# Routing that takes up a group's places after the next but one is finalised, and expert rows gathered four slots ahead

## What is computed

```python
x = x + gnn(layernorm(x), edges) + mix(layernorm(x))
y = layernorm(x)
logits = y @ gate_w + gate_b                      # [6250, 16]
topk_vals, topk_idx = top_k(logits, 2)
topk_w = softmax(topk_vals)
h = relu(y @ w1[e] + b1[e])                       # w1[e]: 256 x 512
expert_out = h @ w2[e] + b2[e]                    # w2[e]: 512 x 256
moe = sum(topk_w * expert_out of the two chosen)
x = x + layernorm(y + moe) * gamma + beta
```

## Time and profile before

| | |
|---|---|
| median of three executions | 2920.93 us |
| the profiled execution: its time, its span | 2916.77 us, 2915.0 us |
| TensorE matmul busy | 1810.2 us, 62% of the span |
| TensorE weight load busy | 1281.5 us, 44% |
| VectorE busy | 1755.7 us, 60% |
| ScalarE busy | 1404.4 us, 48% |
| GpSimd busy | 1329.1 us, 46% |

### The profile page before, as it was taken

One profiled execution on the slowest core, in us unless ns is written; L12 is line 12 of the kernel. 1 busy time (PEld: TensorE's weight loads), 2 busy tenths in 40 slices (PEclk: granted clock), 3 DMA queues, 4 the chain that ended last, 5 costly groups with the idle time before them and its releaser, 6 DMA issues. The chain is left out here.

```text
span 2915.0 us, 41105 instructions
## 1 busy us (share of the span) xinstructions
PE 1810.2 (62%) x8004; PEld 1281.5 (44%) x8005; DVE 1755.7 (60%) x3889; ACT 1404.4 (48%) x4840; POOL 1329.1 (46%) x1298
## 2 busy tenths in 40 slices
PE   3888864554436566666666666663443888888810
PEld 1555443332214344444444444433442788777700
DVE  5886768889635665566656566656442444444368
ACT  1554532223107777778777877783220333333343
POOL 1332200000047777777777777722444444444421
PEclk9999986555666777687777777885555999999955
DMA  4000000000034444444444444415233233223343
GB/s 146 21 21 19 19 8 0 0 0 0 0 93 132 122 132 131 126 125 131 132 124 125 131 125 130 117 44 171 28 68 74 87 90 89 85 88 87 80 165 114
DMA packets 133695, 246.35 MB, mean 85 GB/s; under 512 B 32246, under 2 KB 81702, under 8 KB 133558
## 3 DMA queue, kind: packets, MB, share of 16 engines
q0 software_dynamic: 54288, 141.35, 17.6%
q1 hardware_dynamic: 70112, 93.38, 10.8%
q10 hardware_dynamic: 9158, 10.28, 1.6%
HBM read 209.63 MB, written 35.27 MB: 84 GB/s over the span
## 5 line engine op out<-in xcount | busy, mean ns | idle before, releaser
L1091 POOL DMA_INDIRECT big<-feat_d,idx_a x832 | 830.6, 998 | 261.9 <-issue 260.2
L1123 ACT ACTIVATE big<-big 128x64 f32<-128x64 f32 x3328 | 803.7, 333 | 0.8
L1203 PE MATMUL sums<-big 128*128 128x260 f32 x1664 | 647.7, 511 | 84.5 <-DVE big L1351 52.4
L1351 DVE TENSOR_TENSOR big<-big,sums 128x260 f32 x832 | 352.5, 424 | 317.6 <-PE sums L1203 230.5
L1203 PEld LDWEIGHTS sums<-big 128*128 128x128 f32 x1664 | 338.2, 239 | 202.6 <-ACT big L1123 133.8
L1847 POOL DMA_INDIRECT moe_d<-x_out,x_to x116 | 133.6, 1152 | 245.7 <-DVE x_idx L1886 185.0
L1906 DVE COPY w_sb<-big 128x1024 f32 x116 | 81.5, 703 | 270.5 <-PE p_o L1968 270.5
L1957 PEld LDWEIGHTS p_h<-xT,w_sb 128*128 128x128 f32 x1856 | 228.1, 194 | 6.0
L268 ACT ACTIVATE wgt<-wgt 128x896 f32<-128x896 f32 (+2 forms) x153 | 136.9, 895 | 191.0 <-DVE wgt L540 179.4
L1957 PE MATMUL p_h<-xT,w_sb 128*128 128x128 f32 x1856 | 228.3, 277 | 0.0
L1968 PE MATMUL p_o<-w_sb,hT 128*128 128x256 f32 x928 | 222.3, 383 | 1.1 <-DVE w_sb L1906 1.1
(11 more groups left out here) (356 smaller groups left out, 3062.9 us busy)
## 6 DMA issues: line engine op xcount, KB each, us to landing
big<-code_d SPq DMA_DIRECT2D x52, 512.0 KB
big<-in_L_ffn_w_dram SPq DMA_DIRECT2D x32, 512.0 KB, 10.6
b_sb<-in_L_ffn_b_dram SPq DMA_DIRECT2D x116, 128.0 KB, 3.0
big<-feat_d,idx_a POOLq DMA_INDIRECT x832
big<-moe_d SPq DMA_DIRECT2D x7, 1792.0 KB, 9.9
feat_d<-feat_sb SPq DMA_DIRECT2D x49, 130.0 KB, 2.0
y_d<-Y ACTq DMA_DIRECT2D x7, 896.0 KB, 10.2
X<-in_x_dram SPq DMA_DIRECT2D x6, 1024.0 KB, 17.0
```

The lines of the kernel that those rows point to most:

```text
L1091: nc.gpsimd.indirect_dma_start(out=rows[:, b, lo + s, :], out_offset=None, in_=m["feat_d"], in_offset=bass.IndirectOffsetOnAxis(idx[:, par ...
L1123: ins = nc.scalar.activation(rows[:, b, s, cols], rows[:, b, s, cols], ACT.Copy, scale=rows[:, b, s, HF + h:HF + h + 1])
L1203: nc.tensor.matmul(sums[s % RING][:, 0:HF + H], onehot[:, s // GP % 2, s % GP, :], rows[:, b, s, :], start=True, stop=True).then_inc(summe ...
L1351: nc.vector.tensor_tensor(of, of, sums[s % RING][:, 0:HF + H], ALU.add).then_inc(added, 1)
```

## The change

In routing, `choose(g)` is cut in two: the part behind `chosen` becomes `put(g)`. VectorE finalises two groups ahead: `choose(g)`, `finish(g + 2)`, `put(g)`, `scales(g + 2)`. ScalarE takes the exponential of group g - 2 ahead of the square root of group g. In the experts' stage GpSimd's step for slot k gathers for slot k + 4, and four gathers come ahead of the first step.

```diff
@@ finish_and_route, scalar
             for g in range(GROUPS):
+                if g >= 2:
+                    weigh(g - 2)
                 roots(g)
-                if g:
-                    weigh(g - 1)
                 normalise(g)
                 copies(g)
+            weigh(GROUPS - 2)
             weigh(GROUPS - 1)
@@ finish_and_route, vector
                 dve.sem_inc(chosen, 1)
+
+            def put(g):
+
+                par = g % 2
                 t = slice(g * GT, (g + 1) * GT)
                 dve.wait_ge(weight, g + 1)
...
-            finish(0)
-            scales(0)
+            for g in range(2):
+                finish(g)
+                scales(g)
+            dve.wait_ge(g_in, 32)
+            dve.wait_ge(made, 9)
             for g in range(GROUPS):
-                if g == 0:
-                    dve.wait_ge(g_in, 32)
-                    dve.wait_ge(made, 9)
-                if g + 1 < GROUPS:
-                    finish(g + 1)
-                    scales(g + 1)
                 choose(g)
+                if g + 2 < GROUPS:
+                    finish(g + 2)
+                put(g)
+                if g + 2 < GROUPS:
+                    scales(g + 2)
@@ experts, gpsimd
             def step(slot, w, turn):
-                if there(slot + 3):
-                    gather(slot + 3, (w + 3) % WB)
+                if there(slot + WB):
+                    gather(slot + WB, w)
                 wait_apart(pool, out_ready, slot + 1, passed)
...
-            for slot in range(3):
+            for slot in range(WB):
                 gather(slot, slot)
             walk(pool, step)
```

## The result

The changed kernel takes 2757.27 us in the median of four executions (2753.72 to 2758.06), the kernel before 2920.52 us. The ratio is 0.9441, with a 95% interval of 0.9427 to 0.9456. The forecast was 2757. The profiled execution has a span of 2751.9 us, 163.1 us shorter than before. (In the changed kernel the lines from L1584 on have other numbers: L1602 is L1603, L1620 is L1621, L1713 is L1718, L1946 is L1953.)

A forecast was written before the change was run, and what follows sets the result against it. Routing was bound by a chain between engines, the experts' stage by TensorE with waits on a gather loop. 73.6 + 89.7 = 163.3 us off 2916.8 gave 2753.5, plus 4.2 for the median: 2757 us, range 2735 to 2795.

The forecast's parts named there:

- Routing's turn: Routing, one group's start on TensorE to the next: 20.9 us in place of 34.7, saving 73.6 us.
- the table load of the square root: Routing, ScalarE: runs behind the exponential's load before finalised sums come, costed at nothing; uncovered, 1.3 us each.
- the cover: Routing, VectorE: choosing, finalising and shares, 16.3 us after the scales, fit before the ranks at 18.4; two us spare.
- a pitch of 3.75: Experts' stage: time per slot once gathers go one slot further ahead, in place of 4.53; saves 89.7 us.
- the shown wait of 69.6 us: Experts' stage: TensorE's 81 waits for gathered rows; lower bound of the saving, the upper being 92 us.
- The rival of 3.92: Experts' stage, second rival: only the waiting goes, pitch 3.92 us, 20 us more, 2777 us; chance 10%.
- The loop with one, two and three slots: Experts' stage: chain gather, landing, output takes 9.23 us; serving three slots instead of two, 3.08 us each.
- GpSimd's backlog: Routing: scatters need 21.0 us for a turn of 20.9, about 0.1 us a group; taken as 0, 3 us kept for range.
- the weight loads move forward: Routing, SP's queue: loads after the last finalising move forward about as far as the experts' stage, so their slack stays.
- The clock in routing: Routing, first rival: TensorE's clock rises, VectorE sets the turn at 18.9 us, 2742 to 2747 us; chance 8%.
- The third rival: Experts' stage: VectorE's two weight copies hold GpSimd 0.7 us each, slot 4.5 us, about 2838 us; chance 4%.
- The slower rival: Both stages: more gathers and scatters in flight make gathers land later; 2947 us at 5.4 us a slot; chance 2%.

The follow-up runs named there:

- the runs with a turn of 30.86 us: Changed kernel, ranks taken up before finalising: 2808.34 us; kernel before, exponential of group g-1 moved behind ScalarE's copies of group g: 2895.02 us.
- the second profile: Profile of the changed kernel run again, unedited, as the ruler for the runs beside it: 2759.61 us, ratio 0.9440.
- the next edit: Changed kernel with a group's ranks made by two matmuls over 112 columns in place of fourteen over 16: 2755.49 us, ratio 0.9436.

## Why the prediction was right

**The loops were read right.** The mechanism came out as forecast, and so did its terms. That the median meets the forecast to 0.3 us is luck: the executions of the changed kernel lie between 2752.48 and 2764.44 us. The sum took the median to lie 4.2 us above the profiled execution; it lay 3.6 us above it in the first measurement and 4.8 below it in the second.

Routing's turn was forecast at 20.9 us and is 20.97. Its terms show in the timeline above: VectorE waits 2.26 us for the ranks where 2 were to spare, the clock stayed at 0.50, and the table load of the square root stayed covered. From TensorE's first start to its last transpose 73.3 us went, of the 73.6 forecast. That the cover was finalising and choosing, and not merely an order two groups ahead, was argued from one turn of the trace; the runs with a turn of 30.86 us show it, and split the gain into 3.9 and 9.9.

**The experts' stage.** 89.7 us were forecast, from a pitch of 3.75; the transposes take 521.0 - 430.6 = 90.4 us less. That the shown wait of 69.6 us was the lower bound and not the gain also came out: beside the wait, 21.3 us of TensorE's busy time went too. The prediction put this down to the fill and drain of the array; the size is shown, that cause isn't isolated. The rival of 3.92 would have given 20 us less. The loop with one, two and three slots in it is shown by three pitches.

**GpSimd's backlog** was taken at nothing, with 3 us for the range. It is at nothing, but by a hair: GpSimd goes from one group's last scatter to the next group's first with no more than its 0.3 us, and its rate is the turn's (2036.48, 2057.46, 2078.45, 2099.43, 20.98 apart). With the ranks in two matmuls, where it waits for nothing, four groups take it 83.6 us (2016.80 to 2100.42), 20.9 each, so it could hardly have gone faster. The range had a cause here: by an estimate from these rows, one more stretched scatter in a group (1.75 us instead of 0.96) would have made each such turn 0.8 us longer.

**The step that failed** (without harm to the forecast) is the sentence that the weight loads move forward with the stage that needs them, so that their slack stays. The loads had their slack. But they share the DMA engines with the list's scatters, and I had not asked who else lands there. In the profiled execution this cost 0.6 us (5.52 against 4.89) and was lost in the sum; in the other profiles with the short routing and the loads at the end 2 to 6 us. Loading by group takes the landing back to 4.3 us. Why these seven loads last longer in the changed kernel (the last was issued at 2128.8, 38 us after the first, and 46 us in the second profile; before it was 33) wasn't isolated.

**The rivals.** The clock in routing: 0.50 at 14.89 us busy of 20.90, the level of 1.2 GHz. By the clock gate's rule in the Trainium skill ("TensorE: Matmul & The Clock Gate", part on the clock gate) sustained activity should have raised it, and here it did not rise. That idling lowers it, the other half of the rule, agrees with the gathers two ahead, where TensorE waited 4.7 us in each slot and the mean granted clock was 0.80 instead of 0.99. The third rival, GpSimd held by copies, has a true mechanism: without the copies its instructions are 0.2 us shorter in the mean. The price was 0.2 us for an instruction instead of the 0.7 of a whole copy, and without the copies the time was the same. That a copy locks GpSimd out, as "SBUF — State Buffer" of the Trainium skill has it (the trap that VectorE seems to block DMA), agrees with this in kind. The slower rival didn't come near: the gathers' median landing went from 2.8 to 3.1 us.

The sum, term by term: 73.3 + 90.4 - 0.6 = 163.1, the span's 163.1 us.

## What to carry to other kernels

Where no engine is full, write down one turn of the loop as a chain of times, with the number of items that it serves: a transfer issued one item further ahead divides the chain by one more, until the next engine's own work is the larger number. Take that number from a turn without a wait, not from the time minus the waits: here the waits showed 69.6 us and their removal gave 90. Then ask of each queue that is moved forward what else lands on the same engines at its new time, and look which engine stands second: here three stood within 2 us, so the next edit, 2.4 us off a turn on TensorE, moved the last scatter by less than 5 us in all.

## What the runs showed of the hardware

- GpSimd needs 0.96 us to issue an indirect DMA of 128 rows and 0.30 between two that wait for nothing. Beside VectorE's instructions over 1792 elements with two inputs (2.0 us each) three of them take 2.67, 1.75 and 1.75 us (the first of the three 1.9 to 2.2 us in the first group), in each group whose scatters run beside finalising.
- Beside VectorE's copies of 1024 elements (0.69 us) they take up to 1.3 to 1.4 us, 0.2 more in the mean.
- The scatters' landing goes with what else is in flight: 3.9 to 6.1 us after the last one where the DMA engines' busy share in the 10 us before was 0.02 to 0.09 (eight profiles), and 8.1 to 11.1 us at a share of 0.76 to 0.86 (three profiles). Moving the weight loads away brought it to 4.3 and 4.1.
- TensorE stays at a granted 0.50 (1.2 GHz) in the turns of routing, though in one stretch it is busy for 13.73 us of 13.80 (matmuls of 16 columns and some transposes of 128); in the experts' stage it has 0.99, and with 4.7 us waits in every slot 0.80, where a down-projection behind such a wait takes 3.2 us instead of 1.9.
